# A decoder layer on one NeuronCore: two transposes of each head go from TensorE to DMA transposes of half words, and the sum with the skip term from VectorE to GpSimd

## The chip, the cores and the metric

One NeuronCore of a Trainium2 chip runs the whole layer in one launch. The metric is the device time of one execution in microseconds (us); lower is better. The engines are named as in the profile: PE (TensorE, matmuls and transposes), DVE (VectorE), ACT (ScalarE), POOL (GpSimd) and SP (SyncE, which only issues transfers). Each engine works through its own queue in the order in which the program was written; between engines they wait for one another on semaphores.

## The reference

x is 16 x 256 x 512 (batch, position, channel). Three blocks follow one another, each with a residual and a layer norm ahead of it:

```
x = x + attention(layernorm(x))      # 16 heads, causal, quantised activations, ternary weights
x = x + longconv(layernorm(x), ctx)  # 32 heads of 8 positions
x = x + ffn(layernorm(x))            # silu(gate) * up, then down; inner width 1536

# longconv, for a head h: v = layernorm(x), c = ctx, both 16 batches x 8 positions x 512 channels
kv[i, j, :] = v[i, :] * c[j, :]                          # all 64 pairs, channel by channel
y = causal_convolution(kv, k[h]) + kv * skip[h]          # along the 512 channels
out[j, :] = sum over i of y[i, j, :] * c[i, :]
```

## The kernel before

Part 1 (to about 490 us) is the attention, with an x1 of 16 x 256 x 512 kept in DRAM. It is not touched, except that 4 semaphores instead of 8 now count the loads of x. Part 2 does the long convolution and the feed-forward network together and is what the change is about.

**Heads.** Part 2 goes through the 32 heads of the long convolution. A head's rows are 16 batches x 8 positions = 128 rows, one to a partition. For the convolution along the channels these must lie on the partitions, so c and the normalised v are turned: `turn_c` and `turn_v` on PE (L595, L666) make four 128x128 f32 transposes each into a PSUM bank, and ACT copies the bank out (`copy_cT` L1391 into cT, `prepare` k == 3 at L1484 into vT). kv blocks 0 and 1 are multiplied on DVE (L1084), blocks 2 and 3 on POOL (L1682). The convolution is a product with 128x128 Toeplitz blocks. From head 5 on, sums of kv blocks (kv_sum, kv12 on POOL) give "shared" products on PE (`mix_shared` L689), which ACT copies to SBUF (`copy_shared` L1491) and DVE adds into y (L1114). DVE multiplies y by c into z (L1116) and reduces over i into oT (L1120). The skip term is c times a reduced g_skip (c_skip, POOL L1728); `add_skip` (L1096) adds it to oT on DVE. `turn_back` on PE (L722) turns oT, and `add_mixed` on DVE (L1123) adds it to the residual x_grp.

**Steps.** All engines run the same loop over steps g; a head takes 8 of them (h, s = divmod(g, 8)). In step s of head h PE mixes one of 8 half rows of head h, the other engines follow, and `prepare(h + 1, s)` prepares the next head: s = 0 statistics, s = 1 shift, s = 2 v_sb on ACT and the turn of c, s = 3 the turn of v, s = 4 and 5 kv on DVE, s = 6 kv_sum, s = 7 kv on POOL.

**Groups.** Four heads make a group for the feed-forward network. `norm(gi, k)` begins two steps after the group's last head (GROUP_NORM_AT): DVE's statistics, a power on POOL, the shift on DVE, fn and fnh on ACT, fnl on POOL. Then SP turns fnh and fnl for each of the four tiles into fT with DMA transposes of 128x512 half words (`turn_fn` L1906, L1911). Seven steps after the norm begins, PE's units start, one a step: 24 gate and up products (L749), then 8 half down products (L763). A unit waits for all eight transfers into fT. yo (L1169 on DVE, L1760 on POOL, the store L1916 on SP) is the output of a tile; its two buffers come free when the store has landed. For the last group PE turns fn itself (L736).

**SP's queue** in a head: at s = 4 the loads of x_grp, c_sb and the taps for head h + 2 (L1888, L1834, L1839); at group boundaries turn_fn and the stores.

## Time and profile before

| | us |
|---|---|
| median of 3 runs | 1523.86 |
| lowest, highest | 1521.88, 1523.87 |
| profiled execution, its own time | 1525.19 |
| span in that profile | 1523.4 |
| PE busy | 1423.3 (93%) |
| DVE busy | 1311.2 (86%) |
| POOL busy | 1123.8 (74%) |
| ACT busy | 745.9 (49%) |

Times in the profile run from the span's start. The heads' work lies between about 490 and 1430 us, the last group's feed-forward after it. "Busy" counts a matmul from its start to its modelled end, and matmuls overlap, so on PE the distance between starts says more than the durations. "x8" at a row's end is how many instructions it merges.

### The profile page before, as it was taken

What the parts mean: (1) busy time and instruction counts of PE and PEld (TensorE: products, weight loads), DVE (VectorE), ACT (ScalarE), POOL (GpSimd) and SP (SyncE); (2) the same over time, 40 slices, a digit from 0 to 9 for tenths busy, and PEclk for the clock granted to TensorE, in tenths of its full rate; (3) what the DMA queues carried; (4) which work ended last, traced back from release to release, by engine and by line L of the source; (5) the groups of instructions that cost most, each with busy time, mean ns of one, the idle gap of its engine ahead of it and who ended that gap; (6) DMA issues with size and microseconds to landing.
All of it is one profiled execution on the core that took longest, in us unless ns stands there. A gap on an engine that the chain in (4) does not pass through costs nothing.

```text
span 1523.4 us, 23984 instructions
## 1 busy us (share of the span) xinstructions
PE 1423.3 (93%) x8639; PEld 809.4 (53%) x8717; DVE 1311.2 (86%) x2018; ACT 745.9 (49%) x1334; POOL 1123.8 (74%) x818
## 2 busy tenths in 40 slices
PE   3589999999985987999999999999999999999998
PEld 2477788887863443444444444444444444444443
DVE  5789999999874999899999999999899999999611
ACT  3689999999875112333243333333333333423331
POOL 2379999999985786767776777767876877677432
PEclk9799999999997999999999999999999999999999
DMA  4546455554612522110201300210220121020001
GB/s 141 140 129 160 136 163 149 149 158 127 155 64 77 164 73 62 32 42 25 73 22 35 83 22 21 78 40 21 56 63 21 38 60 42 16 75 1 8 22 28
DMA packets 89217, 113.12 MB, mean 74 GB/s; under 512 B 38132, under 2 KB 42380, under 8 KB 89100
## 3 DMA queue, kind: packets, MB, share of 16 engines
q1 hardware_dynamic: 88908, 111.45, 26.2%
q8 instruction: 70, 1.15, 0.3%
q10 hardware_dynamic: 192, 0.14, 0.1%
q14 instruction: 47, 0.39, 0.1%
HBM read 50.67 MB, written 19.92 MB: 46 GB/s over the span
## 4 chain that ended last, share of the span: by engine, by line
PE 66%; DVE 14%; ACT 7%; POOL 6%; issue 6%; DMA 1%; POOLq 0%; SPq 0%; DVEq 0%; ACTq 0%
PE gu L749 21%; PE gu L763 10%; PE shared_bank L694 9%; PE y L713 3%; PE y L710 3%; PE y L718 3%; PE y L716 3%; PE y L719 3%; POOL pL L1610 3%; DVE blockmax L878 2%; DVE z L1116 2%; DVE o_sb L918 1%; ACT pH L1323 1%; DVE qkt L858 1%; PE s_kq L544 1%
## 5 line engine op out<-in xcount | busy, mean ns | idle before, releaser
L1496 ACT ACTIVATE shared<-shared_bank 128x512 f32<-128x512 f32 x162 | 96.6, 597 | 439.6 <-PE shared_bank L694 439.6
L1114 DVE TENSOR_TENSOR y<-shared,y 128x512 f32<-128x512 f32 x324 | 223.9, 691 | 7.4 <-PE y L719 1.7
L1610 POOL TENSOR_TENSOR pL<-pT,pH 128x768 f16<-128x768 f32 x128 | 216.6, 1694 | 12.1 <-ACT pH L1323 5.8
L1736 POOL TENSOR_TENSOR fuL<-fu,fuH 128x512 f16<-128x512 f32 x96 | 116.7, 1215 | 122.8 <-ACT fuH L1511 122.8
L1120 DVE TENSOR_REDUCE oT<-z 128x64 f32<-128x512 f32 x256 | 175.6, 686 | 8.7
L749 PE MATMUL gu<-fT,wg 128*128 128x512 f16 x768 | 181.4, 379 | 0.0
L749 PE MATMUL gu<-fT,wu 128*128 128x512 f16 x768 | 181.4, 379 | 0.0
L1116 DVE TENSOR_TENSOR z<-y,cT 128x512 f32<-128x512 f32 x236 | 162.2, 687 | 7.2 <-PE y L708 1.6
L1682 POOL TENSOR_TENSOR kv<-vT,cT 128x1024 f32<-128x1024 f32 x70 | 144.5, 2066 | 6.6 <-ACT vT L1489 6.6
L763 PE MATMUL gu<-wd,fuH 128*128 128x512 f16 x384 | 145.5, 379 | 0.0
L763 PE MATMUL gu<-wd,fuL 128*128 128x512 f16 x384 | 145.5, 379 | 0.0
L749 PEld LDWEIGHTS gu<-fT,wg 128*128 128x128 f16 x768 | 75.1, 98 | 118.9 <-issue 47.4
L749 PEld LDWEIGHTS gu<-fT,wu 128*128 128x128 f16 x768 | 75.1, 98 | 106.4 <-issue 35.1
L1317 ACT ACTIVATE pT<-s_kq,ws 128x768 f32<-128x768 f32 x128 | 114.9, 898 | 25.3 <-PE s_kq L558 21.1
L878 DVE TENSOR_REDUCE blockmax<-s_qk 128x6 f32<-128x768 f32 x128 | 121.3, 948 | 5.7 <-PE s_qk L528 4.3
L1603 POOL TENSOR_TENSOR qkhl<-qkt,qkhl 128x512 f16<-128x512 f32 x64 | 86.0, 1345 | 42.2 <-ACT qkhl L1303 42.2
L694 PE MATMUL shared_bank<-kv_sum,toep 128*128 128x512 f32 x216 | 110.5, 593 | 1.7 <-POOL kv_sum L1670 1.7
L1670 POOL TENSOR_TENSOR kv_sum<-kv 128x1024 f32<-128x1024 f32 x27 | 63.5, 2353 | 60.9 <-DVE kv L1084 60.9
L544 PE MATMUL s_kq<-pack 128*128 128x128 f16 x768 | 100.0, 220 | 4.3 <-ACT pT L1317 1.5
L1135 DVE SCALAR_TENSOR_TENSOR fu<-gu,cols,sil 128x512 f32<-128x512 f32 x96 | 71.3, 743 | 33.6 <-PE gu L749 33.6
L1323 ACT ACTIVATE pH<-pT 128x768 f16<-128x768 f32 x112 | 94.0, 839 | 0.0
L544 PEld LDWEIGHTS s_kq<-pack 128*128 128x128 f16 x768 | 75.8, 99 | 18.4 <-issue 0.6
(208 smaller groups left out, 3494.4 us busy)
## 6 DMA issues: line engine op xcount, KB each, us to landing
pack<-qkhl SPq DMA_DIRECT2D x256, 128.0 KB, 2.4
x_sb<-in_x SPq DMA_DIRECT2D x16, 512.0 KB, 4.3
c_sb<-in_ctx SPq DMA_DIRECT2D x32, 256.0 KB, 3.5
hankel<-in_L_xattn_k SPq DMA_DIRECT2D x32, 256.0 KB, 4.0
out_y<-yo SPq DMA_DIRECT2D x32, 256.0 KB, 2.8
x_grp<-x_scratch SPq DMA_DIRECT2D x30, 256.0 KB, 3.4
x_scratch<-x_sb SPq DMA_DIRECT2D x14, 512.0 KB, 2.9
wraw<-in_L_attn_w_qkv SPq DMA_DIRECT2D x3, 1024.0 KB, 9.7
```

Of the source, the lines that this page charges most:

```text
L544: T.matmul(to, pack[:, 1, r, g, key * P:(key + 1) * P], pack[:, 0, r, g, query * P:(query + 1) * P], start=first, stop=False)
L694: T.matmul(shared_bank[:], tap(h, (2, 0, 1)[part]), (kv_sum, kv12, kv_sum)[part][:, half * HB:(half + 1) * HB, :, :].rearrange("p b j i -> ...
L749: made = T.matmul(bank[:], (wg, wu)[which][:, cb, ib * P:(ib + 1) * P], fT[:, cb, part, :], start=cb == 0 and part == 0, stop=cb == CB - 1 ...
L763: made = T.matmul(bank[:], src[:, t * P:(t + 1) * P], wd[:, ib, :], start=ib == 0 and part == 0, stop=ib == IB - 1 and part == 1)
L878: V.tensor_reduce(out=blockmax[b % 2][:, p, :], in_=s_qk[:, 0:6, :], op=ALU.max, axis=AXIS.X, negate=True).then_inc(max_done, 1)
L1114: chain.step(V.tensor_tensor(bank[:], shared[2 * part + half][:], bank[:], op))
L1116: V.tensor_tensor(z[n % 2][:], y, weight, ALU.mult).then_inc(m_zm, 1)
L1120: V.tensor_reduce(out=oT[h % 2][:, lb, own].rearrange("p (b j) -> p b j", b=HB), in_=z[n % 2][:], op=ALU.add, axis=AXIS.X).then_inc(m_z, 1)
L1317: S.activation(pT[n % NP][:], s_kq[:, 0:6, :], ACT.Exp, scale=ws[:, 4:5]).then_inc(exp_done, 1)
L1610: G.tensor_tensor(pL[n % 2][:], pT[n % NP][:], pH[n % NP][:], ALU.subtract).then_inc(low_done, 1)
L1682: G.tensor_tensor(block(h, lb), vT[:, lb, :].rearrange("p (b i) -> p b i", b=B).unsqueeze(2).broadcast_to([P, B, M_POS, M_POS]), cT[h % 2] ...
L1736: G.tensor_tensor(fuL[ib][:], fu[n % 2][:], fuH[:, ib, :], ALU.subtract).then_inc(f_fl, 1)
```

## The change

- For heads 2 to 31 c, and for heads 5 to 31 v, are no longer turned on PE. ACT splits the f32 words into their low and high half words (`split_c`, `split_v`, into the new tile planes, 128 x 2 x 512), one DMA transpose of 128x1024 half words turns both planes at once (`turn_c`, `turn_v` on SP, into c_sb and v_sb), and ACT joins the half words again into cT or vT (`join_c`, `join_v`). Every number stays bit for bit what it was.
- c of head h + 2 is split at the end of step 6 of head h, turned at step 7 and joined in step 2 of head h + 1. v of head h + 1 is made in step 1, split and turned in step 2, joined in step 3.
- planes and c_sb are single, so waits tie them: a split waits until the last turn has read planes, and the load of c for the head after waits for the join.
- `add_skip` goes to POOL, in step 1, behind kv block 3. turn_back moves from step 2 to step 3 and add_mixed from 2 to 4; in the norm the last head's statistics, and with them shift, fn, fnh, fnl and the turns, move one step later. The units start where they did.
- z has one buffer instead of two (its place pays for planes), with a wait for the reduction before it.

```diff
+        planes = q("planes", [P, 2, L], I16)
-        z = [q(f"z{i}", [P, HB, M_POS, M_POS], F32) for i in range(2)]
+        z = q("z", [P, HB, M_POS, M_POS], F32)
...
+        C_TURNED_FROM, V_TURNED_FROM = 2, 5
+        def planes_read(w, heads):
+            if heads > V_TURNED_FROM:
+                w.wait_ge(m_vturned, 16 * (heads - V_TURNED_FROM))
+        def words(tile):
+            return tile.bitcast(I16).rearrange("p (n s) -> p n s", s=2)
         def back_at(h):
-            return 4 if h < GROUP else 2
+            return 4 if h < GROUP else 3
...
 # PE
             def prepare(h, k):
-                if k == 2 and h > 0:
+                if k == 2 and 0 < h < C_TURNED_FROM:
                     turn_c(h, misc2)
-                if k == 3:
+                if k == 3 and h < V_TURNED_FROM:
                     turn_v(h)
...
 # DVE
-                V.tensor_tensor(z[n % 2][:], y, weight, ALU.mult).then_inc(m_zm, 1)
+                w.wait_ge(m_z, n)
+                V.tensor_tensor(z[:], y, weight, ALU.mult).then_inc(m_zm, 1)
...
-                if k in (0, 1):
+                if k in (0, 1, 2):
-                    for t in (2 * k, 2 * k + 1):
+                    for t in ((0, 1), (2,), (3,))[k]:
...
-                if g == MIX_STEPS or (s == 1 and 1 <= h < M_HEADS):
-                    add_skip(h - 1)
-                if g == MIX_STEPS or (1 <= h < M_HEADS and s == back_at(h)):
+                if g == MIX_STEPS or (1 <= h < M_HEADS and s == back_at(h) + 1):
                     add_mixed(h - 1)
...
 # ACT
+            def split_c(h):
+                w.wait_ge(m_cin, 16 * (h + 1))
+                if h > C_TURNED_FROM:
+                    w.wait_ge(m_cturned, 16 * (h - C_TURNED_FROM))
+                planes_read(w, h)
+                S.activation(planes[:].rearrange("p s n -> p n s"), words(c_sb[:]), ACT.Copy).then_inc(m_csplit, 1)
+            def split_v(h):
+                w.wait_ge(m_v, h + 1)
+                w.wait_ge(m_cturned, 16 * (h - C_TURNED_FROM + 1))
+                S.activation(planes[:].rearrange("p s n -> p n s"), words(v_sb[:]), ACT.Copy).then_inc(m_vsplit, 1)
+            def join_v(h):
+                w.wait_ge(m_vturned, 16 * (h - V_TURNED_FROM + 1))
+                w.wait_ge(m_kv, kv_counts(h)[0])
+                w.wait_ge(m_kvp, kv_counts(h)[1])
+                S.activation(words(vT[:].rearrange("p a b -> p (a b)")),
+                             v_sb[:].bitcast(I16).rearrange("p (s n) -> p n s", s=2), ACT.Copy).then_inc(m_vT, 1)
...
 # POOL
+            def add_skip(h):
+                w.wait_ge(m_ck, h + 1)
+                w.wait_ge(m_z, 2 * LB * (h + 1))
+                G.tensor_tensor(oT[h % 2][:], oT[h % 2][:], c_skip[:], ALU.add).then_inc(m_oc, 1)
...
 # SP
             def load_ctx(h):
-                w.wait_ge(m_ctr, h)
+                if h <= C_TURNED_FROM:
+                    w.wait_ge(m_ctr, h)
+                else:
+                    w.wait_ge(m_cT, h)
...
+            def turn_v(h):
+                w.wait_ge(m_vsplit, h - V_TURNED_FROM + 1)
+                Y.dma_start(v_sb[:].bitcast(I16).rearrange("p (g n) -> p g n", n=P),
+                            planes[:].rearrange("p s n -> p (s n)"), transpose=True).then_inc(m_vturned, 16)
+                if s == 7 and C_TURNED_FROM <= h + 2 < M_HEADS:
+                    turn_c(h + 2)
+                if s == 2 and V_TURNED_FROM <= h + 1 < M_HEADS:
+                    turn_v(h + 1)
```

`turn_c`, `join_c` and the rest follow the same pattern. Three places show what moves.

ACT's queue before, over steps 2 to 4 of a head whose PE steps hold gate and up products (v_sb, cT and vT belong to the next head):

```order
L1496 ACTIVATE shared<-shared_bank 128x512 x2
L1511 ACTIVATE fuH<-fu 128x512
L1504 ACTIVATE sil<-gu,cols 128x512
L1481 ACTIVATE v_sb<-x_grp,mstat 128x512
L1396 ACTIVATE cT<-misc 128x512
L1496 ACTIVATE shared<-shared_bank 128x512
L1489 ACTIVATE vT<-misc 128x512
```

The same stretch now:

```order
L1542 ACTIVATE shared<-shared_bank 128x512
L1494 ACTIVATE v_sb<-x_grp,mstat 128x512
L1542 ACTIVATE shared<-shared_bank 128x512
L1557 ACTIVATE fuH<-fu 128x512
L1550 ACTIVATE sil<-gu,cols 128x512
L1521 ACTIVATE planes<-v_sb 128x512x2
L1534 ACTIVATE cT<-c_sb 128x1024
L1542 ACTIVATE shared<-shared_bank 128x512
L1527 ACTIVATE vT<-v_sb 128x1024
```

v_sb went one step ahead, and the split stands where it stood; the copies out of PSUM became joins of twice the length.

SP's queue before, at a boundary between groups:

```order
L1911 DMA_TRANSPOSE fT<-fnh 128x4x128
L1911 DMA_TRANSPOSE fT<-fnl 128x4x128
L1911 DMA_TRANSPOSE fT<-fnh 128x4x128
L1911 DMA_TRANSPOSE fT<-fnl 128x4x128
L1911 DMA_TRANSPOSE fT<-fnh 128x4x128
L1911 DMA_TRANSPOSE fT<-fnl 128x4x128
L1911 DMA_TRANSPOSE fT<-fnh 128x4x128
L1911 DMA_TRANSPOSE fT<-fnl 128x4x128
L1916 DMA out_y<-yo 16x8x512 x4
```

And now:

```order
L1969 DMA_TRANSPOSE fT<-fnh 128x4x128
L1969 DMA_TRANSPOSE fT<-fnl 128x4x128
L1969 DMA_TRANSPOSE fT<-fnh 128x4x128
L1969 DMA_TRANSPOSE fT<-fnl 128x4x128
L1984 DMA out_y<-yo 16x8x512
L1978 DMA_TRANSPOSE c_sb<-planes 128x8x128
L1969 DMA_TRANSPOSE fT<-fnh 128x4x128
L1969 DMA_TRANSPOSE fT<-fnl 128x4x128
L1969 DMA_TRANSPOSE fT<-fnh 128x4x128
L1969 DMA_TRANSPOSE fT<-fnl 128x4x128
L1984 DMA out_y<-yo 16x8x512
L1973 DMA_TRANSPOSE v_sb<-planes 128x8x128
```

A store and the turn of c now stand between the two halves of the turns into fT, which all begin a step later.

DVE's queue before, at the same boundary, from the last statistics to the shift (L1156):

```order
L1153 TENSOR_SCALAR fstat<-fstat 128x4
L1114 TENSOR_TENSOR y<-shared,y 128x512 x2
L1116 TENSOR_TENSOR z<-y,cT 128x512
L1120 TENSOR_REDUCE oT<-z 128x64
L1169 TENSOR_TENSOR yo<-gu,down_bc 128x512
L1156 SCALAR_TENSOR_TENSOR fstat<-fstat 128x4
```

And now (L1168 is the shift):

```order
L1181 TENSOR_TENSOR yo<-gu,down_bc 128x512
L1160 BN_STATS fstat<-x_grp 128x6
L1162 BN_AGGR fstat<-fstat 128x2
L1165 TENSOR_SCALAR fstat<-fstat 128x4
L1100 TENSOR_TENSOR kv<-vT,cT 128x1024
L1125 TENSOR_TENSOR y<-shared,y 128x512 x2
L1128 TENSOR_TENSOR z<-y,cT 128x512
L1132 TENSOR_REDUCE oT<-z 128x64
L1181 TENSOR_TENSOR yo<-gu,down_bc 128x512
L1168 SCALAR_TENSOR_TENSOR fstat<-fstat 128x4
```

The shift, which stood behind the first yo, now stands behind the second and behind the first kv.

## Rows read from the trace of the kernel before

**Rows 1.** page, part 1: engine, busy us (share of the span), instructions.
```profile
PE 1423.3 (93%) x8639; PEld 809.4 (53%) x8717; DVE 1311.2 (86%) x2018; ACT 745.9 (49%) x1334; POOL 1123.8 (74%) x818
```

**Rows 2.** windows: busy us of PE, PEld, DVE, ACT, POOL; PEclk, DMA share, GB/s.
```profile
1000.00:1100.00 100.00, 100.00 (x380) 46.83 (x379) 93.72 (x142) 35.38 (x59) 76.48 (x56) 1.00 0.15 35
```

**Rows 3.** waits of the weight loads, 600 to 1420 us: total us, times, longest.
```profile
PEld gu L749 <- DMA fT<-fnl: 0.8, 1, 0.8
```

**Rows 4.** timeline of PE: start us, duration us, engine, line, operation.
```profile
1010.71 1.02 PE L713 MATMUL y<-kv,toep_own 128*128 128x512 f32 x2
...
1014.59 0.60 PE L599 MATMUL misc<-ident,c_sb 128*128 128x128 f32 x4
1015.03 1.02 PE L713 MATMUL y<-kv,toep_own 128*128 128x512 f32 x2
...
1018.91 1.02 PE L716 MATMUL y<-kv,toep_own 128*128 128x512 f32 x2
...
1022.35 1.02 PE L716 MATMUL y<-kv,toep_own 128*128 128x512 f32 x2
...
1036.13 1.02 PE L710 MATMUL y<-kv,toep 128*128 128x512 f32 x2
```

**Rows 5.** DVE, line L1099: count, duration ns min/median/max, first and last start.
```profile
L1099 DVE TENSOR_TENSOR oT<-oT,c_skip x32: 679/1853/2504, 520.1 to 1429.8; 128x512 f32<-128x512 f32 x32
```

**Rows 6.** timeline of ACT in the head of rows 4.
```profile
1014.21 0.81 ACT L1481 ACTIVATE v_sb<-x_grp,mstat 128x512 f32<-128x512 f32 x1
...
1019.11 0.60 ACT L1489 ACTIVATE vT<-misc 128x512 f32<-128x512 f32 x1 [1.57 <-PE misc L670]
```

**Rows 7.** ACT, line L1534: count, duration ns min/median/max.
```profile
L1534 ACT ACTIVATE fT<-misc x4: 1017/1021/1024, 1450.3 to 1454.3; 128x1024 f16<-128x1024 f16 x4
```

**Rows 8.** timeline of SP's queue at a group boundary.
```profile
963.91 1.26 SPq L1911 DMA_TRANSPOSE fT<-fnh  x1
...
973.07 1.27 SPq L1911 DMA_TRANSPOSE fT<-fnl  x1
```

**Rows 9.** the transfers of line L1911, all 56, from issue to landing.
```profile
DMA to landing us min/median/max: 2.4/2.4/4.2
```

**Rows 10.** timeline of DVE, head of rows 4.
```profile
1020.50 1.21 DVE L1084 TENSOR_TENSOR kv<-vT,cT 128x1024 f32<-128x1024 f32 x1
...
1034.46 0.69 DVE L1116 TENSOR_TENSOR z<-y,cT 128x512 f32<-128x512 f32 x1
```

**Rows 11.** timeline of POOL at the boundary of rows 7.
```profile
965.09 2.18 POOL L1760 TENSOR_TENSOR yo<-yo,x_grp 128x512 f32<-128x512 f32 x1
```

**Rows 12.** timeline of POOL, head of rows 4.
```profile
1014.71 0.46 POOL L1714 TENSOR_TENSOR toep_own<-toep 128x128 f32<-128x128 f32 x1
```

**Rows 13.** timeline of DVE at the boundary of rows 7.
```profile
960.35 0.15 DVE L1156 SCALAR_TENSOR_TENSOR fstat<-fstat 128x4 f32<-128x4 f32 x1
...
964.33 0.68 DVE L1169 TENSOR_TENSOR yo<-gu,down_bc 128x512 f32<-128x512 f32 x1
```

**Rows 14.** timeline of PE at the same boundary.
```profile
980.12 1.89 PE L749 MATMUL gu<-fT,wg 128*128 128x512 f16 x8
```

**Rows 15.** timeline of SP's queue at the first group's boundary.
```profile
608.11 1.27 SPq L1911 DMA_TRANSPOSE fT<-fnl  x1
```

**Rows 16.** timeline of PE at the first group's boundary.
```profile
610.59 1.90 PE L749 MATMUL gu<-fT,wg 128*128 128x512 f16 x8
...
614.88 1.12 PE L694 MATMUL shared_bank<-kv,toep 128*128 128x512 f32 x2 [1.16 <-POOL kv L1705]
```

**Rows 17.** timeline of PE at the end of the heads' work.
```profile
1430.59 0.63 PE L726 MATMUL misc<-ident,oT 128*128 128x128 f32 x4 [2.12 <-DVE oT L1099]
...
1449.65 0.38 PE L736 MATMUL misc<-ident_h,fnh 128*128 128x128 f16 x4 [0.30 <-POOL fnl L1749]
```

**Rows 18.** timeline of DVE at the end of the heads' work.
```profile
1441.79 0.15 DVE L1156 SCALAR_TENSOR_TENSOR fstat<-fstat 128x4 f32<-128x4 f32 x1
1443.34 0.69 DVE L1169 TENSOR_TENSOR yo<-gu,down_bc 128x512 f32<-128x512 f32 x1 [1.40 <-PE gu L763]
```

More of the change, by code:

```diff
@@ L1094, in sum_skip @@
                 V.tensor_reduce(out=g_skip[:], in_=kv_skip[:], op=ALU.add, axis=AXIS.X).then_inc(m_g, 1)
-            def add_skip(h):
-                w.wait_ge(m_ck, h + 1)
-                w.wait_ge(m_z, 2 * LB * (h + 1))
-                V.tensor_tensor(oT[h % 2][:], oT[h % 2][:], c_skip[:], ALU.add).then_inc(m_oc, 1)
             def weigh_sum(n):
@@ L1476, in prepare @@
                     turn_taps(h)
-                elif k == 2:
+                if k == (2 if h < V_TURNED_FROM else 1):
                     xs, sm = x_grp[h // GROUP % 3][:, h % GROUP, :], mstat[h % 2]
                     w.wait_ge(m_shift, h + 1)
-                    w.wait_ge(m_vtr, h)
+                    if h < V_TURNED_FROM:
+                        w.wait_ge(m_vtr, h)
+                    else:
+                        w.wait_ge(m_vT, h)
                     S.activation(v_sb[:], xs, ACT.Identity, bias=sm[:, 9:10], scale=sm[:, 8:9]).then_inc(m_v, 1)
-                    if h > 0:
+                if k == 2:
+                    if h >= V_TURNED_FROM:
+                        split_v(h)
+                    if h >= C_TURNED_FROM:
+                        join_c(h)
+                    elif h > 0:
                         copy_cT(h, misc2)
+                if k == 3 and h >= V_TURNED_FROM:
+                    join_v(h)
                 elif k == 3:
@@ L1489, in prepare, with join_c @@
                     S.activation(vT[:].rearrange("p a b -> p (a b)"), misc2.of["vT", h][:], ACT.Copy).then_inc(m_vT, 1)
+            def split_c(h):
[14 more added lines that the diff above has]
+                             v_sb[:].bitcast(I16).rearrange("p (s n) -> p n s", s=2), ACT.Copy).then_inc(m_vT, 1)
+            def join_c(h):
+                w.wait_ge(m_cturned, 16 * (h - C_TURNED_FROM + 1))
+                w.wait_ge(m_z, 2 * LB * (h - 1))
+                w.wait_ge(m_ck, h - 1)
+                S.activation(words(cT[h % 2][:].rearrange("p a b -> p (a b)")),
+                             c_sb[:].bitcast(I16).rearrange("p (s n) -> p n s", s=2), ACT.Copy).then_inc(m_cT, 1)
             def copy_shared(h, s):
@@ L1515, in norm @@
                 rstd, shift = sm[:, 6 + 2 * GROUP:6 + 3 * GROUP], sm[:, 6 + 3 * GROUP:6 + 4 * GROUP]
-                if k in (2, 3):
-                    for t in (2 * (k - 2), 2 * (k - 2) + 1):
+                if k in (3, 4):
+                    for t in (2 * (k - 3), 2 * (k - 3) + 1):
                         n = GROUP * gi + t
@@ L1557, in scalar_program @@
                     prepare(h + 1, s)
+                if s == 6 and C_TURNED_FROM <= h + 2 < M_HEADS:
+                    split_c(h + 2)
         def gpsimd_program(gpsimd):
@@ L1742, in norm @@
                     G.tensor_tensor(rstd, rstd, minus_half[:, 0:GROUP], ALU.pow).then_inc(f_rstd, 1)
-                elif k in (3, 4):
-                    for t in (2 * (k - 3), 2 * (k - 3) + 1):
+                elif k in (4, 5):
+                    for t in (2 * (k - 4), 2 * (k - 4) + 1):
                         n = GROUP * gi + t
@@ L1775, in gpsimd_program @@
                     within(h, s)
+                if g == MIX_STEPS or (s == 1 and 1 <= h < M_HEADS):
+                    add_skip(h - 1)
                 if s == 7 and h < M_HEADS:
@@ L1911, in turn_fn, with turn_c @@
                     Y.dma_start(fT[:, :, part, t * P:(t + 1) * P], src[:, t, :], transpose=True).then_inc(f_turned, 16)
+            def turn_v(h):
+                w.wait_ge(m_vsplit, h - V_TURNED_FROM + 1)
+                Y.dma_start(v_sb[:].bitcast(I16).rearrange("p (g n) -> p g n", n=P),
+                            planes[:].rearrange("p s n -> p (s n)"), transpose=True).then_inc(m_vturned, 16)
+            def turn_c(h):
+                w.wait_ge(m_csplit, h - C_TURNED_FROM + 1)
+                Y.dma_start(c_sb[:].bitcast(I16).rearrange("p (g n) -> p g n", n=P),
+                            planes[:].rearrange("p s n -> p (s n)"), transpose=True).then_inc(m_cturned, 16)
             def store_out(gi, t):
@@ L1941, in sync_program @@
                 for gi, k in groups(g, GROUP_NORM_AT, NORM_STEPS):
[L1942 to L1944 removed]
+                    if k in (4, 5) and gi < GROUPS - 1:
+                        turn_fn(gi, 2 * (k - 4))
+                        turn_fn(gi, 2 * (k - 4) + 1)
                 for gi, u in groups(g, UNIT_AT, UNIT_STEPS):
```

20 lines of the change are left out of this document (10 added, 10 removed).

## The prediction

> **What bounds the kernel now.** I read the page's table of engines first [rows 1]: TensorE (PE) is busy for 93% of the span, VectorE (DVE) for 86%, GpSimd (POOL) for 74%, ScalarE (ACT) for 49%. An average over stages does not say who waits, so the windows come next. In the hundred microseconds of [rows 2], inside the heads' work, PE is busy 100.00 of 100 us and DVE 93.7, at the full granted clock (1.00). Then the list of waits: in the heads' work nearly all that PE's weight loads wait for is their own issue, 0.3 us at a time at most, and the one wait for a transfer in 820 us, 0.8 us, is at the first boundary between groups of heads [rows 3]. So in the heads' work every instruction taken from PE's queue is time, as long as DVE (6% of slack) and the transfers keep up.
>
> PE's timeline gives the price. A head has 8 steps. In [rows 4] a step without transposes lasts 1022.35 - 1018.91 = 3.44 us; the one that turns v lasts 1018.91 - 1015.03 = 3.88; the one from 1010.71 to 1015.03, with two turns (o back and c), 4.32. One turn of four 128x128 f32 blocks costs PE's queue 0.44 us, whatever the record of 0.60 says, since it overlaps the next matmuls.
>
> **What leaves PE and DVE.** Context c is turned by transfers for heads 2 to 31 (30 turns), v for heads 5 to 31 (27). Two of these 57, both for head 5, stand in head 4, where PE waits for DVE anyway. 55 x 0.44 = 24.2 us is the gain. It also moves the end of each head 0.88 us nearer, so everything that was hidden by less than that must be looked at. From DVE goes the add of c_skip, 0.68 to 2.50 us, 1.85 in the median [rows 5], so of 0.937 x 28.84 = 27.0 us of work in a head without down products (8 x 3.44 + 3 x 0.44 = 28.84 on PE) 25.2 are left, beside PE's 27.96. The single z adds a wait for DVE's own last write before a multiply. Most multiplies have an add into y ahead of them, so I take nothing; the bound above is 0.1 us on two of eight multiplies.
>
> **v's round trip.** Before, v_sb starts on ACT at 1014.21, PE turns it and vT starts at 1019.11 [rows 6]. Now v_sb is made a step earlier, and a split of 1024 half words stands where v_sb stood. No row shows ACT reading or writing single half words that lie 1024 bytes apart. The nearest is the copy of 128x1024 f16 in 1.02 us [rows 7]; below it stands the 0.60 of a 512-wide copy [rows 6], above it I allow double, 2.04. I take 1.02. The transfer: SP's queue issues 128x512 half words in 1.26 us and eight of them one behind the other at 1.30 each, (973.07 - 963.91)/7 [rows 8]; they land 2.4 us after their start [rows 9]. Twice the size gives 2.5 us of issue and 2.4 + 1.26 = 3.7 to landing; bounds 2.4 and 4.8. So vT is ready at 1014.21 + 1.02 + 0.1 + 3.7 + 1.02 = 1020.05 (0.1 is an allowance for SP to start). DVE began kv at 1020.50 and ended the eighth z at 1034.46 + 0.69 = 1035.15 [rows 10], 14.65 us later; now 1034.7. PE's second step of the next head, which needs that z, stood at 1036.13 [rows 4] and is now due at 1036.13 - 0.88 = 1035.25. There are 0.55 us to spare, so this costs nothing, but each microsecond beyond costs one in each of the 21 heads whose PE steps hold no down products (27 hosts less the six with them). Behind split and join on ACT wait the copies of the shared products, and PE's next shared product waits for the copy of the last. Split, join and copy are 2.64 us of a step of 3.44, and every second step has two more ACT instructions of some 0.6 (fuH and the silu); that is full, but for one step only. I put nothing there, and up to 0.3 us a head into rival three.
>
> Where the trace is silent, the Trainium skill, page "SBUF — State Buffer", section "Door 1: The DMA port swizzle", says that SBUF is read in lines of 16 bytes and that an access pattern which goes to a new line at each element pays. By it the splits and joins would be slow; no row here shows such an access. That is rival two below, and the price there is worked out from rows. The page "DMA: Bandwidth & Descriptors", section "Latency and other measured facts", gives 261 GB/s for transposing transfers, by which the second 128 KB would add 0.5 us and not 1.26, and the sum would lose about 0.8 at each boundary. Of trains of short ones the rows say otherwise: 128 KB each 1.30 us, paced by issue [rows 8].
>
> **POOL.** It takes on the add: between the 0.68 of DVE's shortest [rows 5] and the 2.18 of the same shape on POOL beside a busy DVE [rows 11]; I take 1.9. Queued behind it are a fuL, the third sum of kv and the last toep_own, which PE needs in its step 4. That one started at 1014.71 and took 0.46 [rows 12]; 1017.1 with 1.9 more, against PE's 1018.91 - 0.88 = 1018.03. Hidden by 0.9 us. The turn back of o now stands one step later on PE and finds its add done.
>
> **The group boundary.** This is the cost. The norm's last statistics move one step later, because the head's result reaches x_grp a step later. On DVE the shift started at 960.35; now it stands behind the second yo, which was at 964.33 [rows 13] and is at most 0.88 earlier for PE's sake and up to 0.9 more for DVE's own relief. The shift comes at 963.2 to 964.1. SP's first transfer started 963.91 - 960.35 = 3.56 us behind it; so now 966.8 to 967.6. In SP's queue the four issues of tiles 0 and 1 (5.2 us) are followed by a store (0.5), by the new turn of c (2.5) and by four issues, the last of which starts 3.9 after the first. The last starts at 978.9 to 979.7 and lands at 981.3 to 982.1. PE's gate product, which was at 980.12 [rows 14] with its data there since 975.5, is now due at 979.24. PE waits 2.1 to 2.9 us; I take 2.4, and 6 x 2.4 = 14.4 for groups 1 to 6. The store of the second yo comes late too and holds DVE's fourth yo until about 985; PE is then late already, so I add nothing. At the first boundary the last transfer started at 608.11 [rows 15], landed at 610.5, and PE went at 610.59 [rows 16]. The turn of c adds 2.5 and the later shift something between 0 and a step of 3.4, less the add that leaves DVE: 1.6. Of 4.1 the wait of 1.16 for POOL at 614.88 [rows 16] goes: 2.8.
>
> **The end.** PE's last turn back waited 2.12 us for DVE's add [rows 17]; on POOL, alone there, it takes some 0.5 more. The shift at 1441.79 now stands behind the second yo at 1443.34 [rows 18], which is 2.3 later or 2.8 with the 0.5. PE's transposes of fnh started at 1449.65 after only 0.30 of waiting [rows 17]. 2.8 less what ACT and POOL had in hand: 2.0, bounds 0.5 and 2.8.
>
> **The sum.** -24.2 + 14.4 + 2.8 + 2.0 = -5.0. The profiled execution took 1525.2 us, 1.3 over the median shown, so 1520.2 for it and 1518.9 for the median: 1519.
>
> **The rivals.** One: the boundary is nearly free, because the long transpose issues faster than twice the short one or the shift comes in DVE's old lag. For it: the data had 980.12 - 975.5 = 4.6 us in hand at this boundary. Against: the eight issues fill 10.4 us by themselves. With 0 to 0.8 us at each of six, -24.2 + 2.4 + 2.8 + 2.0 = -17, so 1507; with all of it free, 1500. Two, on the other side: v's round trip comes late. If split and join take double, vT is ready at 1014.21 + 2.04 + 0.1 + 3.7 + 2.04 = 1022.1, 1.5 past the point where PE waits: 21 x 1.5 = 32, so 1519 + 32 = 1551. It decides from 1020.6 on, and turns the whole change slower from about 0.25 us past that. For it: no row shows the access, and only 0.55 us are to spare; against: ACT's duration follows the number of elements in all rows I have, [rows 6, 7]. With both bounds of the transfer taken too, 1573. Three: small new waits (POOL's last toep_own hidden by 0.9, DVE's z, SP's queue) take 0.1 to 0.3 us a head, 3 to 8 us in all: within the noise, 1524.
>
> **Chances.** The forecast 0.38 (its own range 1514 to 1523), rival one 0.18, rival two 0.26, rival three 0.18. A measurement of this kernel can tell about 0.2%, 3.0 us, from no change. Faster by more: rival one and most of the forecast, 0.52. Within: the rest of the forecast, most of rival three, 0.20. Slower: rival two and a little of three, 0.28. The range takes in rival one but its extreme and the lower two thirds of rival two: 1501 to 1546.
>
> **What would show it.** PE's steps with the turns of c and v at 3.44 us; if they are longer by other waits, the gain is not there. In a head of group phase: vT ready before DVE's kv; if DVE waits for ACT's vT there, rival two. The durations of the ACT lines on planes: 1.02 or near 2. The new transfers' issue: 2.5 us on SP's queue. At each of six boundaries PE's gate product waits about 2.4 us for fT; without that wait, rival one. The turn back waits for POOL at the end only. The forecast is wrong if the transfers of half words are cheaper or dearer than twice the short ones, since both the round trip and the boundary hang on that.

## The result, and the profile after

The changed kernel takes 1608.24 us in the median (1604.36 to 1611.47, four runs), the kernel before 1523.18 (1521.88 to 1523.87, four runs beside them): 1.0558 times as long, with a 95% interval of 1.0542 to 1.0574. The forecast was 1519 with a range to 1546. The profiled execution took 1604.4 us, its span is 1602.6.

The page of the changed kernel, part 1 and the first line of part 4 (the chain that ended last), stands against [rows 1]:

```profile
PE 1429.3 (89%) x8489; PEld 786.3 (49%) x8489; DVE 1288.4 (80%) x1986; ACT 1032.6 (64%) x1391; POOL 1155.9 (72%) x850
...
PE 29%; DVE 26%; ACT 19%; issue 14%; POOL 8%; SPq 2%; DMA 2%; POOLq 0%; DVEq 0%; ACTq 0%
```

PE's busy time hardly moved, its share fell, and ACT's busy time rose by 287 us with 57 instructions more. The hundred microseconds of [rows 2], in the changed kernel (windows; busy us of PE, PEld, DVE, ACT, POOL):

```profile
1000.00:1100.00 100.00, 89.97 (x313) 39.52 (x312) 80.89 (x120) 63.60 (x64) 69.49 (x52) 0.98 0.24 61
```

PE was busy for 100 of these, DVE for 93.7; now no engine is full, so waits between engines set the time there. The groups of ACT's instructions from 640 to 1500 us show what is slow (busy us, mean ns | idle before, releaser):

```profile
L1521 ACT ACTIVATE planes<-v_sb 128x1024 int16<-128x1024 int16 x25 | 119.6, 4784 | 0.0
L1516 ACT ACTIVATE planes<-c_sb 128x1024 int16<-128x1024 int16 x25 | 119.0, 4761 | 0.0
...
L1534 ACT ACTIVATE cT<-c_sb 128x1024 int16<-128x1024 int16 x25 | 36.0, 1440 | 0.0
L1527 ACT ACTIVATE vT<-v_sb 128x1024 int16<-128x1024 int16 x25 | 29.4, 1174 | 34.1 <-DMA v_sb<-planes 34.1
```

A split, which writes half words alternately to two places 1024 bytes apart, takes 4.8 us. A join, which reads from two places as far apart and writes in sequence, takes 1.2 to 1.4. The waits of the same stretch (total us, times, longest):

```profile
DVE y L1125 <- ACT shared L1542: 71.7, 28, 3.7
...
PEld gu L765 <- DMA fT<-fnl: 30.6, 6, 5.1
PEld y L734 <- DVE z L1128: 28.7, 38, 1.4
PE shared_bank L710 <- ACT shared L1542: 26.3, 19, 1.6
PE gu L765 <- DMA fT<-fnl: 25.6, 6, 4.3
```

One head shows how the first of them comes about. ACT's timeline in the changed kernel:

```profile
1052.14 0.81 ACT L1494 ACTIVATE v_sb<-x_grp,mstat 128x512 f32<-128x512 f32 x1 [2.22 <-DVE mstat L1092]
...
1054.43 4.80 ACT L1521 ACTIVATE planes<-v_sb 128x1024 int16<-128x1024 int16 x1
1058.71 1.45 ACT L1534 ACTIVATE cT<-c_sb 128x1024 int16<-128x1024 int16 x1
1060.04 0.61 ACT L1542 ACTIVATE shared<-shared_bank 128x512 f32<-128x512 f32 x1
1062.01 1.17 ACT L1527 ACTIVATE vT<-v_sb 128x1024 int16<-128x1024 int16 x1 [1.36 <-DMA v_sb<-planes]
```

and DVE's, with the instruction that waits for that copy and the product that reads vT:

```profile
1050.81 1.30 DVE L1092 SCALAR_TENSOR_TENSOR mstat<-mstat 128x1 f32<-128x1 f32 x1
...
1056.79 0.69 DVE L1125 TENSOR_TENSOR y<-shared,y 128x512 f32<-128x512 f32 x1
1060.75 0.70 DVE L1125 TENSOR_TENSOR y<-shared,y 128x512 f32<-128x512 f32 x1 [3.28 <-ACT shared L1542]
...
1063.40 1.22 DVE L1100 TENSOR_TENSOR kv<-vT,cT 128x1024 f32<-128x1024 f32 x1
```

DVE itself releases ACT's v_sb (by mstat, at 1052.1). Behind v_sb stand the split of v, the join of c and the copy of a shared product, which DVE could use 5.4 us after that release (1057.5) and gets after 8.6. v_sb of the next head hangs on DVE's own order again, so I read the 3.28 us as a loop that is paid once a head; experiment 4 tests it. Down the line vT is ready at 1063.18 and kv starts at 1063.40, so v's own round trip is as late: by these rows DVE without the wait would have come to kv at 1060.1 and stood there for some 3.1 us. No run moves the copy ahead of the split, so the two are not told apart; both stand behind the same split.

At a boundary of groups, SP's queue and then PE (start us, us):

```profile
1007.12 0.60 SPq L1984 DMA_DIRECT2D out_y<-yo  x1
1009.47 1.26 SPq L1978 DMA_TRANSPOSE c_sb<-planes  x1
1010.77 1.26 SPq L1969 DMA_TRANSPOSE fT<-fnh  x1
```

```profile
1017.16 2.52 PE L765 MATMUL gu<-fT,wg 128*128 128x512 f16 x8 [4.28 <-DMA fT<-fnl]
1019.47 1.91 PE L729 MATMUL y<-kv,toep_own 128*128 128x512 f32 x2
```

The turn of c waits in SP's queue for the end of its split (the queue is free from 1007.72 to 1009.47), and four transfers of fT wait behind it. PE's gate waits 4.28 us, where it waited for nothing at [rows 14]. Then its granted clock falls, in windows of PE alone:

```profile
1012.00:1017.00 5.00, 0.89 (x3) 1.00 0.47 105
...
1018.00:1022.00 4.00, 4.00 (x9) 0.57 0.07 25
```

The 1.91 us at 1019.47 are those of two matmuls that take 1.02 at the full clock [rows 4]. The engine had been idle from 1012.9 to 1017.2; by 1022 the clock was at 1.00 again.

A measure for all that follows is the start of c_skip on GpSimd, once a head. Four heads are a cycle, with one boundary in it. From the cycle's end behind the first boundary to that of five cycles later, c_skip starts at 727.08 and 1339.41 before: 122.5 us a cycle. After, 738.29 and 1404.97: 133.3. So the five cycles account for 54 of the span's 79 us. The cycle of the first boundary (119.5 before, 135.0 after) adds 16, the last three heads (84.0, 92.6) 9, the end behind the last c_skip (100.0, 105.0) 5; the time ahead of the first of these starts is 4 less, and differs by up to 4 among kernels that do nearly the same there.

### The profile page after: what moved, and what is told of

Its sections match the earlier page's. It is cut to its first block, busy times and chain, and to the rows that moved or that the text cites. A ratio compares the mean times of both kernels' runs of the same rounds, so it can differ in the third digit from the quotient of the medians.

```text
span 1602.6 us, 23994 instructions
## 1 busy us (share of the span) xinstructions
PE 1429.3 (89%) x8489; PEld 786.3 (49%) x8489; DVE 1288.4 (80%) x1986; ACT 1032.6 (64%) x1391; POOL 1155.9 (72%) x850
## 4 chain that ended last, share of the span: by engine, by line
PE 29%; DVE 26%; ACT 19%; issue 14%; POOL 8%; SPq 2%; DMA 2%; POOLq 0%; DVEq 0%; ACTq 0%
PE gu L765 8%; DVE y L1125 6%; DVE z L1128 5%; ACT planes L1521 4%; PE gu L779 3%; PE shared_bank L710 3%; ACT cT L1534 2%; POOL pL L1658 2%; ACT planes L1516 2%; SPq L1969 2%; DVE fu L1147 2%; DVE kv L1100 2%; DVE blockmax L894 1%; DVE o_sb L934 1%; POOL yo L1813 1%
## 5 line engine op out<-in xcount | busy, mean ns | idle before, releaser
L765 PE MATMUL gu<-fT,wg 128*128 128x512 f16 x768 | 188.6, 390 | 31.3 <-DMA fT<-fnl 31.3
L1516 ACT ACTIVATE planes<-c_sb 128x1024 int16<-128x1024 int16 x30 | 142.9, 4763 | 23.9 <-DMA c_sb<-in_ctx 23.9
L1730 POOL TENSOR_TENSOR kv<-vT,cT 128x1024 f32<-128x1024 f32 x70 | 138.5, 1979 | 5.5 <-ACT vT L1509 5.5
L1521 ACT ACTIVATE planes<-v_sb 128x1024 int16<-128x1024 int16 x27 | 129.1, 4782 | 0.0
L1557 ACT ACTIVATE fuH<-fu 128x512 f16<-128x512 f32 x96 | 59.9, 624 | 81.2 <-DVE fu L1147 81.2
```

The source lines that it names most:

```text
L765: made = T.matmul(bank[:], (wg, wu)[which][:, cb, ib * P:(ib + 1) * P], fT[:, cb, part, :], start=cb == 0 and part == 0, stop=cb == CB - 1 ...
L1516: S.activation(planes[:].rearrange("p s n -> p n s"), words(c_sb[:]), ACT.Copy).then_inc(m_csplit, 1)
L1521: S.activation(planes[:].rearrange("p s n -> p n s"), words(v_sb[:]), ACT.Copy).then_inc(m_vsplit, 1)
L1730: G.tensor_tensor(block(h, lb), vT[:, lb, :].rearrange("p (b i) -> p b i", b=B).unsqueeze(2).broadcast_to([P, B, M_POS, M_POS]), cT[h % 2] ...
```

## The experiments

All ratios are to the kernel before, run beside them, with a 95% interval. "Plane by plane" is the same split in another order of its elements: all low half words and then all high ones, so that the output is written in sequence and the input is read at every second half word. A "cycle" is that of the section above.

**1. Both splits plane by plane.**

```diff
-S.activation(planes[:].rearrange("p s n -> p n s"), words(c_sb[:]), ACT.Copy)
+S.activation(planes[:], words(c_sb[:]).rearrange("p n s -> p s n"), ACT.Copy)
```

and the same for v_sb.

> Both splits on ScalarE are written plane by plane (the output is contiguous, the input is read with a stride of one word), nothing else changes. Theory A, the scattered writes: the 4.77 us of a split are the price of writing neighbouring half words 1024 B apart. Then the split takes 1.0 to 1.5 us like the two joins (1.17), VectorE's wait of 3.3 us for the copied shared piece goes, the period of a head with gate and up in it falls from 30.9 to about 28.0 us, the boundaries of the groups lose part of their wait, and the kernel takes about 1512 us (1503 to 1525). Rival B, the half words: ScalarE is slow on two-byte integers that it reads or writes with a stride, in whatever order; the split stays at 4.8 us and the time at about 1608. Rival C, the moves: the splits become short, but the order of the work, not their length, cost the time; then the kernel stays above 1570.

Measured: 1521.66 us, ratio 0.9982 (0.9970 to 0.9994). The splits, from 640 to 1500 us:

```profile
L1521 ACT ACTIVATE planes<-v_sb 128x1024 int16<-128x1024 int16 x25 | 26.3, 1051 | 0.0
L1516 ACT ACTIVATE planes<-c_sb 128x1024 int16<-128x1024 int16 x24 | 25.1, 1045 | 0.0
```

and the waits that answer to those above:

```profile
PE gu L765 <- DMA fT<-fnl: 8.1, 6, 1.4
...
DVE y L1125 <- ACT shared L1542: 5.8, 8, 0.9
```

Two lines on ACT are worth 86.6 us. A cycle takes 120.6 us for 133.3. Rivals B and C fall. I had expected 1512, though: the last c_skip starts only 7.6 us sooner than before (1415.83 for 1423.41), and 4.9 of these go at the end (104.9 for 100.0).

**2. Context and v turned on TensorE again.** `C_TURNED_FROM, V_TURNED_FROM = M_HEADS, M_HEADS` (2, 5).

> All turns of context and v go back to TensorE (no split, no transfer, no join for them); the sum on GpSimd, the turn of the normalised rows by transfers, their norm steps and the single z stay as in the changed kernel. Theory A: the loss came from the splits alone, in the heads and through ScalarE at the boundaries: about 1525 us (1518 to 1533). Rival: the late normalisation and the turn of its rows at the boundary are at fault with their own length: seven boundaries of about 6 us, so 1555 to 1570.

Measured: 1532.46, ratio 1.0061 (1.0046 to 1.0076). A cycle takes 122.4 us, as before, so at these boundaries the later norm, taken with the sum's move off VectorE, costs nothing as long as no other transfer stands in SP's queue. At the first boundary it does: PE waits 2.3 us for fT, and that cycle takes 123.4 for 119.5. The end takes 106.6, 6.6 more than before. The time ahead of the first c_skip of the count is 4.6 less, so that of all this 6.4 are left between the spans (1529.8 and 1523.4).

**3. The context alone, by the scattered split.** `V_TURNED_FROM = M_HEADS` (5).

> v goes back to TensorE; the context is still split by the scattered write, turned and joined. Theory A, by ScalarE's time in the head: one long split a head instead of two. If the two cost alike, the time lies midway between the changed kernel and the one with both turns on TensorE, near 1565. If it is the split of the context that delays the copies of the shared piece (it stands right ahead of them), nearly all the loss stays: 1590 or more. If it is v's, whose result the same head waits for, it goes: below 1540.

Measured: 1547.66, ratio 1.0160 (1.0144 to 1.0175), a cycle 124.3 us. It fits none of the three figures: nearer to "v's", with a loss of its own that sits at the boundaries (33.5 us for the head at 1012, 31.2 with both splits plane by plane).

**4. v alone by the scattered split.** The first line of experiment 1 only.

> The split of the context is written plane by plane, the split of v stays the scattered one (4.8 us); nothing else changes. So of the 87 us between the changed kernel (1608) and the one with both splits plane by plane (1521.7) this shows v's part. Theory A1, v's chain: v is normalised, split, turned and joined within three steps of the same head, so its split delays the copies of the shared pieces behind it on ScalarE and the products that wait for vT; most of the 87 us are v's: 1580 to 1600, with heads of 30 us or more. The context alone cost little (with v on TensorE 1547.7, 15 us above the kernel with neither). Theory A2, ScalarE's queue: only both long splits together overfill a head, and one alone hides: 1525 to 1545.

Measured: 1589.26, ratio 1.0426 (1.0412 to 1.0441), a cycle 131.0 us, with heads of 30.9 as in the changed kernel. So v's split makes the loop of a head: 67.6 us over experiment 1, and c's adds 19, most of it at the boundaries. DVE's wait for the copy of a shared product, 71.7 us in the changed kernel, is 72.6 here (30 times), 12.3 in experiment 3 and 5.8 in experiment 1: it comes and goes with v's long split. One long split a head stands in experiments 3 and 4 alike, so ACT's total load does not do it.

**5. Patterns of copies, ScalarE.** Appended to the changed kernel.

```diff
+bench(planes[:].rearrange("p s n -> p n s"), words(v_sb[:]))
+for step in (1, 2, 4, 8, 16):
+    bench(far[:, 0:352 * step:step], src[:, 0:352])
+bench(flat.rearrange("p (m s k) -> p m k s", s=2, k=4), src.rearrange("p (m k s) -> p m k s", s=2, k=4))
```

> The changed kernel with some 22 ScalarE copies appended at its end, one after the other, each waiting for the one before (its time is of no interest, the durations of the copies are). Eleven patterns of 128 partitions, twice: the split as it is; the split written plane by plane; the join; 352 half words read contiguous and written with steps of 1, 2, 4, 8 and 16 elements; 256 pairs of four-byte words written alternately 1024 B apart; and the split with runs of 4 and of 32 half words a side before it changes sides. Theory A1, each write to another place than the word before costs: the split takes 4.8 us, plane by plane 1.0 to 1.2, the join 1.2; steps of 8 and 16 cost as much a word as the split (352 words, about 1.7 us) and steps of 1 and 2 the normal price (about 0.5 us); runs of 32 about 1.1 us, runs of 4 about 2. Theory A2, only two-byte writes that do not fill a word of four bytes: steps of 2 to 16 all cost the same and more than step 1, and the four-byte words written alternately run at the normal price, about 0.6 us. Rival B: every pattern with two-byte integers costs like the split for each word.

The last two patterns were described wrongly: by this rearrangement they change sides at every half word, to a place 4 (8 bytes) or 32 half words (64 bytes) away. Measured, in order of their first pass: the split, steps of 1, 2, 4, 8 and 16, pairs of four-byte words, then 8 and 64 bytes apart (min/median/max ns, first and last start):

```profile
L1614 ACT ACTIVATE planes<-v_sb x1: 4717/4717/4717, 1603.9 to 1603.9; 128x1024 int16<-128x1024 int16 x1
...
L1614 ACT ACTIVATE fuH<-v_sb x1: 496/496/496, 1610.9 to 1610.9; 128x352 int16<-128x352 int16 x1
L1614 ACT ACTIVATE fuH<-v_sb x1: 593/593/593, 1611.4 to 1611.4; 128x352 int16<-128x352 int16 x1
L1614 ACT ACTIVATE fuH<-v_sb x1: 980/980/980, 1612.1 to 1612.1; 128x352 int16<-128x352 int16 x1
L1614 ACT ACTIVATE fuH<-v_sb x1: 1757/1757/1757, 1613.1 to 1613.1; 128x352 int16<-128x352 int16 x1
L1614 ACT ACTIVATE fuH<-v_sb x1: 1671/1671/1671, 1614.9 to 1614.9; 128x352 int16<-128x352 int16 x1
L1614 ACT ACTIVATE planes<-fu x1: 1087/1087/1087, 1616.6 to 1616.6; 128x512 f32<-128x512 f32 x1
L1614 ACT ACTIVATE planes<-v_sb x1: 1057/1057/1057, 1617.7 to 1617.7; 128x1024 int16<-128x1024 int16 x1
L1614 ACT ACTIVATE planes<-v_sb x1: 4737/4737/4737, 1618.8 to 1618.8; 128x1024 int16<-128x1024 int16 x1
```

The price comes with the place that is written, not with the type: it grows up to a step of 8 half words, which is 16 bytes, and not beyond. (4717 - 1056)/1024 and (1757 - 496)/352 both give 3.6 ns for a half word that lands elsewhere. Alternation to a place 8 bytes away is free (1.057 us for 1.056). A1 stands but for four-byte words: 512 of them, alternated 1024 bytes apart, took 1.09 us where a copy of as many that is read backwards and written in sequence takes 0.63 (toep, L1399). Rival B falls.

**6. More patterns, and the other engines.**

```diff
+bench(w, lambda o, i: S.activation(o, i, ACT.Copy), 0)
+bench(w, lambda o, i: V.tensor_copy(o, i), 12, 8)
+bench(w, lambda o, i: G.tensor_copy(o, i), 20, 8)
```

> The changed kernel with copies appended at its end (their durations matter, not its time): twelve patterns on ScalarE, then the first eight on VectorE and on GpSimd. The patterns: the split as it is, plane by plane, the join; 352 half words written contiguous and with a step of 8; 352 four-byte words written contiguous and with steps of 4 and 8 (16 and 32 bytes); on ScalarE also four-byte words with a step of 2, half words written alternately to places 16 and 32 bytes apart, and 352 half words read with a step of 8. From the first patterns: a half word that goes to another 16 bytes than the one before costs 4.4 ns (4717 less 200 over 1024; 1757 less 200 over 352), any other about 0.8; alternately at 8 bytes apart it is cheap, at 64 bytes it is not. Theory F, partly written words of memory: a four-byte word to another 16 bytes costs far less, 1.7 ns (1086 less 200 over 512), so steps of 4 and 8 take about 0.8 us for 352; alternation 16 bytes apart costs the full 4.7 us; reading with a step of 8 costs nothing more (0.5 us). Rival G, the distance decides whatever the width: 352 four-byte words with a step of 4 or 8 take 1.7 us. For VectorE and GpSimd: if the price is the memory's, the split takes over 3 us there too; if it is ScalarE's own, 0.6 to 1.2 on VectorE and about 2 on GpSimd.

Measured. On VectorE the split and plane by plane; on GpSimd the same; on ScalarE a step of 4 four-byte words, half words alternated 16 bytes apart, and 352 half words read with a step of 8 (busy us, mean ns | idle before):

```profile
L1262 DVE COPY planes<-v_sb 128x1024 int16<-128x1024 int16 x1 | 2.7, 2726 | 21.8 <-ACT planes L1628 21.8
L1262 DVE COPY planes<-v_sb 128x1024 int16<-128x1024 int16 x1 | 0.7, 694 | 0.0
...
L1864 POOL COPY planes<-v_sb 128x1024 int16<-128x1024 int16 x1 | 4.7, 4691 | 27.5 <-DVE fuH L1262 27.5
L1864 POOL COPY planes<-v_sb 128x1024 int16<-128x1024 int16 x1 | 1.0, 1036 | 0.1
...
L1628 ACT ACTIVATE fuH<-fu 128x352 f32<-128x352 f32 x1 | 0.8, 820 | 0.0
...
L1628 ACT ACTIVATE planes<-v_sb 128x1024 int16<-128x1024 int16 x1 | 4.7, 4734 | 0.0
...
L1628 ACT ACTIVATE planes<-fuH 128x352 int16<-128x352 int16 x1 | 0.8, 819 | 0.0
```

F stands for writes: half words 16 bytes apart cost in full, a four-byte word (820 - 496)/352 = 0.9 ns, with 496 ns for the 352 written in sequence. It missed on reads: a step of 16 bytes costs 0.9 ns a half word as well, though the join, which alternates between two streams, pays next to nothing. All three engines pay, VectorE 2.0 ns a half word.

**7. Sum on VectorE and the norm a step earlier.** As in the kernel before, with the turns plane by plane and one z.

```diff
-    G.tensor_tensor(oT[h % 2][:], oT[h % 2][:], c_skip[:], ALU.add).then_inc(m_oc, 1)
+    V.tensor_tensor(oT[h % 2][:], oT[h % 2][:], c_skip[:], ALU.add).then_inc(m_oc, 1)
-return 4 if h < GROUP else 3
+return 4 if h < GROUP else 2
```

and all norm steps back by one.

> Both splits plane by plane, and the sum of outputs and skip term back on VectorE at its old place, with the turn back, the sum with the residual and the norm steps one step earlier, as in the kernel before. What stays of the change: context and v turned by transfers from heads 2 and 5 on, one z. Theory C, the boundary: what kept the plane-by-plane kernel from the gain (1521.7 where its heads run at 27.6 us for 28.8) are the group boundaries (31.2 us for a head that has 27.6 without one) and the end (4.3 us longer than before), both from the rows that are normalised one step later. Then a boundary costs under 1 us, the end is as before, and the kernel takes about 1500 us (1495 to 1506). Rival D, VectorE becomes the bound: the sum's 0.7 us a head and the single z fall on an engine busy 91 to 94% of the heads; heads grow to 28.3 and the kernel takes 1508 to 1516. Rival E: the boundary is a matter of the transfers themselves, which wait for those of the context; then 1515 or more.

Measured: 1530.33, ratio 1.0046 (1.0032 to 1.0059). The boundary was as C had it (29.8 us for heads of 29.2), but the heads were longer than even D said. The same window, and the next experiment's:

```profile
1000.00:1100.00 100.00, 97.64 (x352) 43.56 (x350) 96.98 (x146) 42.95 (x64) 77.22 (x55) 1.00 0.21 51
```

```profile
1000.00:1100.00 100.00, 98.51 (x357) 44.23 (x356) 94.19 (x145) 44.19 (x66) 78.14 (x56) 1.00 0.22 56
```

**8. The same with two z; 9. experiment 1 with two z.**

```diff
-V.tensor_tensor(z[:], y, weight, ALU.mult)
+V.tensor_tensor(z[n % 2][:], y, weight, ALU.mult)
```

> The kernel of before with context and v turned by transfers (plane by plane) and nothing else of the change: sum on VectorE, norm steps as before, and two z. It was 1530.3 with one z, in heads of 29.2 us where 27.6 were left on TensorE. Theory D1, the single z: each product waits for the sum over the product before, which costs VectorE some 0.1 us sixteen times a half head; with two z the heads fall to 27.9 and the kernel takes 1500 to 1508. Theory D2, VectorE's load: the sum's 0.69 us sits in each head and VectorE is full whatever z is; then heads stay at 28.8 or more and the time above 1520.

> Both splits plane by plane, everything else as in the changed kernel, but two z. Its rows show waits of only some 3 us of TensorE for z, so by the sum of waits it gains at most 3: 1518.5 to 1522. Theory D1 with a full VectorE would give 1510 or less.

Measured: 1519.28, ratio 0.9975 (0.9963 to 0.9987), and 1519.54, ratio 0.9978 (0.9966 to 0.9990). A second z is worth 11 us with the sum on VectorE, and with it on GpSimd at most 2, which the intervals don't tell from nothing. Experiment 8 falls between D1 and D2, at heads of 28.2 and 29.2 us in turn. With turns gone from PE and the sum on VectorE, VectorE is next at once (busy 97.0 and 94.2 of the 100 us). The sum's move to GpSimd shortens the heads to 27.6, but with the norm a step later it buys in the heads only what is lost at boundaries and end.

**10. Gate and up one step later.** `NORM_STEPS = 8` (7) on experiment 1.

> Both splits plane by plane, everything else as in the changed kernel, but the gate and up matmuls of each group begin one step (3.4 us) later, so the turned normalised rows have as long to arrive as before. Theory C: six boundaries lose their wait for the turned rows and the fall of the clock behind it, about 3 us each, while the order of the work on TensorE is else the same; the end can lose up to 3.4 us again, as TensorE has less to do beside the last heads. 1505 (1500 to 1512). Rival E: the wait is set by something that moves along (the down matmuls' outputs, the store), and the time stays at 1518 to 1524.

Measured: 1519.89, ratio 0.9977 (0.9966 to 0.9987). PE no longer waits for fT anywhere, but the boundary waits had been 1.3 us each and not the 3 I put in, and small waits for z and for issue (2.9 and 2.6 us in all) took part of their place. So 6.2 us were won by the head at 1325 (1325.21 for 1331.38), 3.9 of them at the first boundary, and 3.5 lost at the end. The forecast of 1505 was missed; the time lies in rival E's band, though its reason does not hold.

**11. An early end; 12. both.** On experiment 1, then with experiment 10's line: the last head's sum on VectorE, and for the last group alone the norm at its old steps.

```diff
+if g == MIX_STEPS:
+    V.tensor_tensor(oT[(h - 1) % 2][:], oT[(h - 1) % 2][:], c_skip[:], ALU.add).then_inc(m_oc, 1)
+early = gi == GROUPS - 1
-elif k == 3:
+elif k == 3 - early:
```

> Both splits plane by plane; the sum with the skip term of the last head alone is on VectorE, and the norm steps of the last group alone come as early as in the kernel before. The end in the plane-by-plane kernel takes 104.9 us from the last c_skip, 100.0 before: 0.6 for the sum on GpSimd, 2.6 for the wait for the last fnl, some 1.7 for the matmuls behind it at half the clock. If these three are the cause, the end is back at 100 us and the kernel at 1517 (1515 to 1519). Rival: the end is late for what went ahead of it (the down matmuls of group 6 are finished too early to cover the chain of the norm), then the wait stays and the time is at 1520 or more.

> The same end, and the gate and up matmuls of every group one step later. The step later won 6.2 us by the head at 1325 (1325.2 for 1331.4) and lost 3.5 at the end, which had waits of its own of 2.7, 3.3 and 2.3 us and matmuls at half the clock. With the earlier norm of the last group the end loses the 4.9 of the other kernel too: 1513 (1510 to 1517). Rival: the end is short of matmuls to cover the norm, one unit of 1.7 us less than without the later step, so that it stays at 107 us or more: 1518 to 1520.

Measured: 1516.54, ratio 0.9957 (0.9942 to 0.9973), with an end of 100.0 us; and 1511.69, ratio 0.9925 (0.9911 to 0.9939), with an end of 102.0. The end's three causes are confirmed as a sum; no run takes them one by one. PE's turn of the last rows, in experiment 1 and in experiment 11:

```profile
1445.28 0.38 PE L752 MATMUL misc<-ident_h,fnh 128*128 128x128 f16 x4 [2.90 <-POOL fnl L1802]
...
1446.20 0.63 PE L779 MATMUL gu<-wd,fuH 128*128 128x512 f16 x1
```

```profile
1440.01 0.39 PE L752 MATMUL misc<-ident_h,fnh 128*128 128x128 f16 x4 [0.31 <-POOL fnl L1810]
```

Experiment 12 is the fastest, 0.75% below the kernel before and 6% below the changed one. In its window of 1000 to 1100 us PE is full again:

```profile
1000.00:1100.00 100.00, 100.00 (x366) 45.88 (x365) 91.44 (x145) 47.08 (x69) 81.11 (x60) 1.00 0.22 57
```

## Why the prediction was wrong

**The step that failed** is the duration of the splits: "The nearest is the copy of 128x1024 f16 in 1.02 us", "above it I allow double, 2.04. I take 1.02". The two splits took 4.76 and 4.78 us, 4.7 times what I took and 2.3 times the bound. With them at 1.05 the kernel takes 1521.66, within the forecast's own range of 1514 to 1523. That it comes so near 1519 is in part luck, since errors cancel: the six boundaries wait 6.3 us less than forecast, the first one waits 1.9 more, the end takes 2.9 more, and some 4 us of the gain are missing (below). The upper bound was no bound: the row it doubled is contiguous on both sides, and no row showed scattered writes. The sentence that the Trainium skill, page "SBUF — State Buffer", section "Door 1: The DMA port swizzle", makes an access pay that goes to a new line of 16 bytes for each element stood in the prediction, and was priced by that doubling. The runs agree with it as to the 16 bytes: 352 half words took 1.76 us at a step of 16 bytes and 1.67 at one of 32, and 1024 of them alternating 8 bytes apart took 1.06. It was also read too widely: the joins were lumped with the splits, and they took 1.17 to 1.44 us.

**Rival two** had the direction, and its limit ("1020.6 on", "turns the whole change slower from about 0.25 us past that") was not far off. By its own formula with the measured pieces, 1014.21 + 4.78 + 0.1 + 2.7 + 1.17 = 1022.96, it gives 2.4 us for each of 21 heads, 50 us, and so 1569 for the measured 1608. Measured were 3.3 in a head (30.9 us for 27.6 in experiment 1) and 5.3 in one with a boundary (36.5 for 31.2). What it missed is the other end of the same delay: the copy of a shared product behind split and join on ACT, which I had called "full, but for one step only" and priced at nothing, with "up to 0.3 us a head" in rival three. That wait is the one that the profile shows, with v's own round trip as late behind it.

**The transfers of 1024 half words**, which I took at 2.5 us of issue and 3.7 to landing, took 1.23 to 1.27 and 2.7 to 2.8 in the median: as long to issue as the 512 [rows 8], 0.3 to 0.4 longer to land [rows 9]. The page "DMA: Bandwidth & Descriptors" of the Trainium skill, section "Latency and other measured facts", has 261 GB/s, for a middle dimension that is not contiguous, and by it the estimate would have been 0.5 more to the landing. That was nearer than mine.

**The boundary** was forecast with 2.4 us of waiting for fT, six times. With short splits it is 8.1/6 = 1.35, which fits a turn of c that occupies SP's queue for 1.3 and not 2.5. With long ones it is 25.6/6 = 4.3 and a stretch at the lower clock, which I had not thought of. At the first boundary the forecast was 2.8 (by its own terms 4.1 - 1.16 = 2.9); experiment 1 waited 4.7 there, the longest of its seven (PE's waits from 600 to 1440 us: total us, times, longest):

```profile
PE gu L765 <- DMA fT<-fnl: 12.8, 7, 4.7
```

**The end** was forecast at 2.0, bounds 0.5 and 2.8, and is 4.9. The waits are 0.6 and 2.6 us longer (2.73 for 2.12 at the turn back, 2.90 for 0.30 at fnh [rows 17]). The rest, 1.7, is eight matmuls behind the second at the lower clock. These are measured in experiment 1; the changed kernel's end is as long, 105.0.

**The turns** went as forecast: a cycle loses 8 x 0.44 = 3.5 us of PE's work, and 122.5 - 3.5 + 1.35 = 120.4, for 120.6 in experiment 1. So did GpSimd's add, 1.27 us against my 1.9: in experiment 1 PE's turn back did not wait for it in the heads' work but at the end. Of -24.2, however, about 4 us are missing in experiment 1: -24.2 and 12.8 of waits for fT would give -11.4 up to the last c_skip, and -7.6 were measured. PE's timeline there places most of them:

```profile
599.26 8.83 PE L724 MATMUL y<-kv,toep 128*128 128x512 f32 x16 [3.02 <-DVE z L1128]
...
616.33 3.29 PE L765 MATMUL gu<-fT,wg 128*128 128x512 f16 x8 [4.71 <-DMA fT<-fnl]
619.41 1.37 PE L729 MATMUL y<-kv,toep_own 128*128 128x512 f32 x2
```

and before:

```profile
598.03 7.13 PE L708 MATMUL y<-kv,toep 128*128 128x512 f32 x16 [1.34 <-DVE z L1116]
```

Ahead of the first boundary PE waits 1.7 us longer for z, which now stands in DVE's queue behind the later steps (the sum with the residual and the last statistics), and the 16 matmuls behind it take 1.7 more, at a granted clock of 0.62 in 600 to 604. Behind the wait of 4.71 the clock falls once more: the eight matmuls take 3.08 from start to start for 1.73 and the next two 1.21 for 0.86, 1.7 in all. Each later wait costs 1.50 between starts and not 1.35, 0.9 in all. These are 6.0 more; three waits of before, of 1.68, 1.16 and 0.39 between 605 and 633, are gone, 3.2 less. That leaves about 1 us open.

**VectorE's relief** I had booked as mere slack. It is more in the heads, and nothing in the whole: with the sum on VectorE the heads are VectorE's (29.2 us with one z, 28.2 and 29.2 with two, for 27.6), but with two z the kernel takes 1519.28 that way and 1519.54 the other (experiments 8 and 9), since the later norm takes the difference back. A single z cost nothing that can be told from zero with the sum on GpSimd, as forecast, and 11 us with it on VectorE.

## What to carry to other kernels

A copy that reorders half words has a good and a bad side to be scattered on: here it paid to write in sequence and read with the stride (1.05 us for 4.77). Time the one access pattern that no row shows before anything is hung on it. When a step has a producer and consumer on the same engine with a second engine between, lateness there can be paid once a round, with no engine full; follow what is queued behind the slow instruction, and not only its own result. When the bound engine is relieved, look at how full the next one is before taking work back to it.

## What the runs showed of the hardware

- Half words written to another 16 bytes than the one before cost 3.6 ns more each on ScalarE and GpSimd (4.72 and 4.69 us for 1024, written in sequence 1.06 and 1.04), 2.0 on VectorE (2.73 for 0.69). Four-byte words so written cost 0.9 ns each on ScalarE. Half words read 16 bytes apart cost 0.9, two alternating streams 0.1.
- A transposing transfer occupies the issuing queue for 1.23 to 1.27 us in the median, with 512 half words a partition or 1024, and lands 2.4 or 2.7 to 2.8 us after its start.
- In the changed kernel TensorE stood idle for 4.28 us, and about a microsecond after work had begun again the granted clock fell to the lower of its two levels (1.2 GHz; 0.57 in the mean of 1018 to 1022) for some 3.5 us, which cost 1.7 us. In experiment 1 the same came behind waits of 3.02, 4.71 and 2.90 us (behind the last, seven matmuls took 0.63 us each for 0.38), in experiment 2 behind one of 2.31 (0.50 in 612 to 614); behind the waits of 1.33 to 1.37 at the later boundaries of experiment 1 it did not (1.00 in 980 to 985).
